# An encoder block of twelve attention units: rows of narrow heads in two halves of the partitions, one pool of PSUM banks, another order of loads and steps

## What is computed

```python
x = x + 0.5 * ffn(layernorm(x)); x = x + attn(layernorm(x)); x = x + 0.5 * ffn(layernorm(x))
# attn: 16 heads of dimension 4, on the left 64 channels
q, k, v = (left @ W.T).reshape(N, S, 16, 4); att = softmax(q k / sqrt(8)); out = (att v) @ Wo.T + bo
# ffn: 16 heads of dimension 8 with rope, then RMS norm, a shared MLP, a group and expert router, 8 experts
q = rope(src @ Wq); k = rope(src @ Wk_c @ Wk); v = src @ Wv_c @ Wv
x = rmsnorm(src + softmax(q k / sqrt(8)) v @ Wo, n1)
h = swiglu(x @ W1_shared); routed = sum_e (h @ W2[e]) * w[:, e]      # w: the best 2 of 4 experts of one group
out = rmsnorm(x + swiglu(x @ W_shared_in) @ W_shared_out + routed, n2)
```

## Time and profile before

| | us |
|---|---|
| median of 3 runs (lowest, highest) | 1025.39 (1023.57, 1027.55) |
| span of the profiled execution | 1017.9 |
| PE busy in it | 914.7 (90%) |
| DVE busy | 716.2 (70%) |
| ACT busy | 536.3 (53%) |
| POOL busy | 349.8 (34%) |
| granted PE clock, mean | 0.947 of 2.4 GHz |

### The profile page before, as it was taken

How to read it: one execution, slowest core, us unless ns; L and a number is a source line. 1 busy time by engine, 2 the same in 40 slices (tenths; PEclk the granted TensorE clock), 3 DMA queues, 4 the chain that set the end, 5 groups by cost and what they waited for, 6 DMA issues and landing times.

```text
span 1017.9 us, 12955 instructions
## 1 busy us (share of the span) xinstructions
PE 914.7 (90%) x4228; PEld 328.1 (32%) x4308; DVE 716.2 (70%) x1344; ACT 536.3 (53%) x1062; POOL 349.8 (34%) x669
## 2 busy tenths in 40 slices
PE   2179988999999999999999999999989999999967
PEld 1022223433433333333322323223233433433333
DVE  6579868768768666865867878778777688683227
ACT  1003755547537545653667666666754367367421
...
GB/s 166 102 80 56 71 61 24 79 30 1 34 13 47 33 8 51 11 27 7 50 42 43 23 96 22 63 67 30 100 2 67 63 13 3 1 13 3 1 10 10
DMA packets 21733, 41.28 MB, mean 41 GB/s; under 512 B 3308, under 2 KB 19500, under 8 KB 20012
## 3 DMA queue, kind: packets, MB, share of 16 engines
...
q10 hardware_dynamic: 240, 0.10, 0.0%
...
## 4 chain that ended last, share of the span: by engine, by line
PE 67%; DMA 9%; DVE 8%; issue 6%; POOL 5%; ACT 4%; SPq 1%; POOLq 0%; ACTq 0%; DVEq 0%
PE ps_max L552 14%; PE ps_out L587 14%; PE ps_exp L574 12%; PE ps L648 9%; PE ps L633 5%; DMA qk_parts<-parts 4%; DMA max_parts_rows<-maxT 3%; DVE maxes L726 2%; ACT probs L884 2%; PE ps L599 2%; DVE src L755 2%; PE ps L534 2%; PE ps L611 1%; PE ps L640 1%; PE ps_max L648 1%
## 5 line engine op out<-in xcount | busy, mean ns | idle before, releaser
L884 ACT ACTIVATE probs<-ps_exp 128x512 f32<-128x512 f32 x768 | 434.6, 594 | 298.4 <-PE ps_exp L574 247.4
L726 DVE TENSOR_REDUCE maxes<-ps_max 128x1 f32<-128x512 f32 x768 | 494.3, 684 | 132.0 <-PE ps_max L552 130.3
L552 PE MATMUL ps_max<-k_aug,q_aug 72*128 72x512 bf16 (+1 forms) x768 | 306.3, 401 | 25.8 <-DMA k_aug<-ones_row 12.5
L574 PE MATMUL ps_exp<-q_aug,k_aug 128*128 128x512 bf16 x688 | 265.7, 389 | 16.3 <-DMA q_aug<-max_parts_rows 9.2
L587 PE MATMUL ps_out<-probs,v_aug 128*9 128x512 f32 x1536 | 204.2, 604 | 4.0 <-ACT probs L884 2.2
L552 PEld LDWEIGHTS ps_max<-k_aug,q_aug 72*128 72x128 bf16 (+1 forms) x768 | 74.7, 98 | 265.9 <-DVE maxes L726 141.9
L574 PEld LDWEIGHTS ps_exp<-q_aug,k_aug 128*128 128x128 bf16 x768 | 74.9, 98 | 181.8 <-ACT probs L884 91.9
L648 PE MATMUL ps<-w,hidden 128*128 128x512 f32 x216 | 101.8, 599 | 0.0
L815 DVE TENSOR_TENSOR prod<-ps,gate 128x512 f32<-128x512 f32 x52 | 36.0, 692 | 55.3 <-PE ps L648 43.4
L1078 POOL TENSOR_TENSOR prod<-prod 128x512 f32<-128x512 f32 x28 | 35.5, 1268 | 97.7 <-DVE prod L815 83.0
L963 POOL TENSOR_SCALAR var_eps<-mean_var 128x4 f32<-128x4 f32 x12 | 2.8, 233 | 162.0 <-DVE mean_var L686 162.0
...
## 6 DMA issues: line engine op xcount, KB each, us to landing
...
qk_parts<-parts SPq DMA_DIRECT2D x48, 128.0 KB, 2.3
...
```

The source lines that it names most:

```text
L552: pe.matmul(ps_max[:, n % MAX_RING, :], q_aug[0:k, r, h, qt * 128:(qt + 1) * 128], k_aug[0:k, r, h, :], start=True, stop=True).then_inc(ma ...
L574: pe.matmul(ps_exp[:, n % EXP_RING, :], k_aug[:, r, h, kt * 128:(kt + 1) * 128], q_aug[:, r, h, :], start=True, stop=True).then_inc(exp_fu ...
L726: dve.tensor_reduce(maxes[:, u % 2, h // HH, qt, h % HH:h % HH + 1], ps_max[:, n % MAX_RING, :], AX.X, ALU.max).then_inc(max_done, 1)
L884: act.activation(probs[:, step % P_RING, c, :], ps_exp[:, n % EXP_RING, :], ACT.Exp, scale=scale).then_inc(exp_done, 1)
```

## The change

- **Banks.** All seven banks besides `ps_out` are one pool. `plan()` gives each step the banks that come free first by a table of holding times (`HOLD`).
- **Row halves.** In an attention unit half of the heads have their rows at partitions 0 to 38 and half at 64 to 102 (`first_row`), and consecutive matmuls change between the halves. `exp_scores` reads product rows plus 3 only, so no row is set to zero.
- **Head order and `v_aug`.** Heads go in groups of four; `v_aug` has 18 columns per head, of which 9 are zero, so two groups add up in one `ps_out`. Per unit there are two evacuations (L892 before) instead of four, and 8 transposes of heads instead of 16. The maxima are transposed in one go per piece, and there are two or four pieces per unit (`EARLY_UNITS`).
- **Loads.** q rows come by one DMA instead of three, k rows by three that each take every third row. For unit 0 they come in four pieces of four heads, k stored and loaded by ACT's queue. The 19 late weights are issued one by one among the steps. Rows of ones are loaded only where they move.
- **Last unit.** Its queries go in two halves; the work after the first half stands among the exponentials of the second.
- **Places.** Every table of places is new, and `MAX_LATE` is a list, one number per unit.

```diff
+def first_row(u, h):
+    return 64 * half_of(u, h)
+def group_head(g, c):
+    return 8 * (g // 2) + 2 * c + g % 2
+MAX_LATE = [39, 33, 23, 14, 16, 18, 22, 24, 25, 21, 15, 18, 14]
+def max_place(u, m):
+    start, end = ((v - 1) * TILES + MAX_LATE[v] for v in (u, u + 1))
+    if u and (is_ffn(u) != is_ffn(u - 1) or u in MAX_PAIRS):
+        m += 1 - m % 2
+    return start + m * (end - start) // TILES
...
+    def take(self, name, u, place):
+        run = max_run(u) if name == "max_scores" else exp_run(u) if name == "exp_scores" else 1
+        n = 2 if name in TWO_BANKS else run if name in HOLD else 0
+        taken = sorted(sorted(range(BANKS), key=lambda i: self.free_at[i])[:n])
...
+            for g, i in itertools.product(range(halves), range(pieces)):
+                r0, at = first_row(u, 2 * g), slice((g + i) * n, (g + i + 1) * n)
...
+                    of = of.rearrange("d c h n -> (d c) h n").unsqueeze(1)
+                    queue.dma_start(q_aug[r0:r0 + rows, r, at, :], of.to_broadcast([PARTS * d, PARTS, n, S])).then_inc(landed, 16)
...
-                    pe.matmul(ps_exp[:, n % EXP_RING, :], k_aug[:, r, h, kt * 128:(kt + 1) * 128],
-                              q_aug[:, r, h, :], start=True, stop=True).then_inc(exp_full, 1)
+                        pe.matmul(bank(use[i]), k_aug[p0:p1, r, at, kt * 128:(kt + 1) * 128],
+                                  q_aug[p0:p1, r, at, :], start=True, stop=True).then_inc(bank_full[use[i][0]], 1)
...
-                        mm = pe.matmul(ps_out[COL * c:COL * c + VW, :], v_aug[:, r, kt, h * VW:(h + 1) * VW],
-                                       probs[:, n % P_RING, c, :], start=(kt == 0), stop=(kt == TT - 1))
+                        mm = pe.matmul(ps_out[COL * c:COL * c + 2 * VW, :], v_aug[:, r, kt, 4 * (g // 2) + c, x0:x0 + 2 * VW],
+                                       probs[:, n % P_RING, c, :], start=first_one, stop=last_one)
...
-                    if u < 2:
-                        if u == 0:
-                            seq(pool.memset(k_aug[64:128, 0:1, :, :].bitcast(F32), 0.0))
```

785 lines of the change are left out of this document (491 added, 294 removed).

## The result

The changed kernel takes 863.53 us (median of 4 runs, 861.74 to 864.27) against 1024.74 us (1023.57 to 1027.55): a ratio of 0.843, 95% interval 0.841 to 0.846. The forecast was 884 us with a range of 862 to 916. The result is faster, as forecast, and lies at the lower edge of the range: the gain is 161 us where 141 were forecast. The profiled execution took 863.97 us, its span is 862.2 us.

A forecast was written before the change was run, and what follows sets the result against it. PE's queue was taken to bound stages 1 to 10, and chains of single steps the opening and tail. Opening, stages and tail summed to 877 us of span; 7.5 more gave 884 us, range 862 to 916.

The forecast's parts named there:

- The span and the runs: Whole kernel: the span lies 7.5 us below the median of the runs, so a span of 877 means 884 us.
- The opening: Before the first exponential: faster row loads and 28 reductions ahead instead of 49 give 47 us instead of 88.3.
- PE's queue: Stages 1 to 10: summed instruction prices on PE give queues such as 78, 76 and 73.5 us for stages 1 to 3.
- The allowance above the queue: Ffn stages carry 2 to 3 us above PE's queue; stages 7 and 8 take 56 and 57 for queues of 51 and 54.
- The wait in stages 1 and 9: Stages 1 and 9: 8 us of waiting for rows behind q loads shrinks, leaving them 3 us above their queues.
- Stages 5 and 6: Attention stages: PE, DVE and ACT each have 40 to 42 us, tied by banks, giving 49 each; ends 43 and 60.
- Rival "evacuation bounds them": Attention stages: evacuation and shared banks hold stages 5 and 6 at 58, 7 and 8 at 59; 910 us, chance 0.15.
- The halves overlap: Pairs of 36-row matmuls in different halves run together, saving 4.9 us in stage 3, 10 in stage 4, 6 in stage 7.
- the rival: Stages 3 to 7: matmuls in different row halves don't overlap; 31 us more, 915 us, chance 0.15.
- Late weights: Stage 0: 19 weights queued among row loads cost nothing, covered by unit 1's early rows; otherwise one wait up to 9.86 us.
- Stage 11 and tail: End of the kernel: stage 11 takes 70 us and the tail 34 instead of 48, together 104 instead of 117.
- The slower case: All 1536 score matmuls wait for planned banks; slower than before above 0.09 us each, 1068 us at 0.12; chance 0.02.

The follow-up runs named there:

- experiment 8: Changed kernel with unit 0's rows loaded whole instead of in four pieces of four heads: 871.12 us against 863.53.
- experiment 7: Changed kernel with the max matmuls of every unit back at 15 places behind the start of the stage before: 956.14 us against 863.53.
- experiments 1 and 2: Changed kernel with both row halves at partition 0: 900.96 us; changed kernel without rounding max matmul places to pairs in units 4 and 8: 883.26 us.
- experiment 6: Changed kernel with the seven banks divided between max scores, exponentials and the rest as in the kernel before: 908.05 us against 863.53.
- experiment 9: Changed kernel with each of the eight transposes of a unit's heads done twice on PE: 869.26 us against 863.53.
- Experiment 10: Changed kernel with every eighth reduction on DVE done twice, the second into a spare column: 889.15 us against 863.53.
- experiment 1: Changed kernel with all narrow heads of attention units at partition 0 instead of half at 64: 900.96 us against 863.53.
- Experiments 3 and 4: Changed kernel with the 19 late weights issued at the very beginning: 859.39 us; changed kernel with them 32 places later: 860.22 us.
- Experiment 5: Changed kernel with the last unit not cut into two halves of its queries, post work at the old places: 879.65 us against 863.53.

## Why the prediction was right, and where it was not

**The span and the runs.** I set the time 7.5 above the span, as in the kernel before. Here run and span differ by 1.8 (863.97 and 862.2), and in 21 later executions of the kernel before by 1.9 to 2.6, so the profiled execution there must have been some 5 us faster than the median. Of the 20 us by which the forecast was high this is 6; the stages give the other 15.

**The opening**, forecast 47 us: 47.0, and the first max matmul at 30.1 for 28. The mechanism holds in both its halves. The store of k parts is slower the more of q loads beside it (experiment 8), and fewer reductions ahead do bring the first exponential forward (15.9 us by experiment 7). The hit to the tenth is luck: the first max matmul came 2.1 us late, and what follows it took 16.9 us where 19 were put. The working led by 28 reductions; 16 and the way of the row stand on the path.

**PE's queue.** The forecast's queue sums for stages 1 to 3 and 7 to 10 are 78, 76, 73.5, 51, 54, 75, 73; measured are 79.4, 77.2, 75.0, 51.8, 53.2, 76.2, 72.7. That is within 1.5 us. Pairs and changes of tile are confirmed in experiments 1 and 2. Stage 4 took 72.7 where the queue had 68 and the forecast 71: in its first 15 us DVE is busy for 14.5 us and PE for 13.2, so there DVE leads, which the forecast had only for stages 5 and 6. One price was wrong: a transpose is 0.11, not 0.22, so the 8 fewer per unit save 0.9 and not 1.8 us a stage. It also makes every sum too long, by 0.9 us for the eight of heads alone, so part of the agreement is two errors that meet; PE's own idle time in these stages is 0.2 to 1.1 us.

**The allowance above the queue.** I put 2 to 3 us on each ffn queue "like stage 2" of before, and 5 and 3 on those of stages 7 and 8. The stages came out between 0.8 below and 1.5 above their sums. This is the term that was mis-sized, and it is what stages 1 to 3 and 7 to 10 came out shorter, 15.5 us (7 and 8 alone 8). With divided banks and all the rest in place the same stages stand 2 to 8 us above the same sums (experiment 6): sharing the banks takes away waits that I had priced at nothing. Experiment 6 puts sharing at 44 us. That is its price with all the rest in place, not a share of the gain: the new order was laid out for shared banks, and in the kernel before, with divided ones, PE waited for a bank for only 1 us or so of stage 2. The same holds for the places (some 90 us in experiment 7). The prices of taking parts away (25, 20, 12, 44, 90 and 8) add up to more than the 161 gained.

**The wait in stages 1 and 9.** I had taken the 8 us of stage 1 above its sum for a wait behind the loads of q rows, and the forecast's drop to 3 above the queue rests on it. The trace of before doesn't bear this out: within stages 1 and 9 PE waits for no DMA. (At the end of stages 7 and 8 it does wait, 2.20 and 3.39 us, for a row of maxima.) What it waits for is VectorE's norm; before, then now:

```profile
166.70 4.47 DVE L755 SCALAR_TENSOR_TENSOR src<-src,rms,n 128x128 f32<-128x128 f32 x4
...
171.23 1.12 PE L618 MATMUL ps<-ident,src 128*128 128x128 f32 x4 [2.49 <-DVE src L755]
```
```profile
126.95 1.12 DVE L1002 SCALAR_TENSOR_TENSOR src<-src,rms,n 128x128 f32<-128x128 f32 x4
```

The four instructions took 4.47 us while POOL worked on 128x512 tiles beside them, and take 1.12 now with POOL idle, as they took 1.14 in the tail of before. Behind the wait of 2.49 us the clock was 0.56 for 7 us, which is 3.1 us of work, and in the first 5 us of stage 1 it was 0.56 too, another 2.2, behind a wait of 3.59 us for a row of maxima at the end of stage 0. The stages came out 1.4 and 1.2 above their sums, less than the 3 forecast, so the size was nearly right and its reason was not: that is luck. No run separates the place of the norm from the other edits.

**Stages 5 and 6**, forecast 49 each: 47.1 and 47.3, with DVE at 89 and 94%. The stages stand 3 to 5 us above DVE's busy time, less than the 7 that I chose between 1 and 18. Rival "evacuation bounds them" was right that PE is not alone there (experiment 9: 0.9 us more on PE lengthens stage 5 by 0.5 and stage 6 not at all) and wrong in the size, 58 us. Experiment 10 can't be read by stage, so what more work on DVE costs there isn't shown.

**The halves overlap.** Forecast at 0.60, the rival at 0.15 with 31 us; experiment 1 measures 25. The Trainium skill's "Measured speedup vs the span model" (page "TensorE: Matmul & The Clock Gate") has 3.07 times for four row tiles; by my estimate from it a pair would have cost 0.29 (the prediction has 0.28). Two starts together, the next two 0.23 us behind them, and stage 7 within 1 us of its queue show no such loss for two halves.

**Late weights.** I took nothing and named the price should the cover go, up to 9.86. The cover I named (unit 1's rows, 28 us ahead of their use) held; what was hit was another thing, the rows of maxima of unit 0, and stage 0 took 62.7 us instead of 56. Experiments 3 and 4 give 5.8 and 5.4 of it back. Both beat the changed kernel; the better is 859.4 us.

**Stage 11 and tail**, forecast 70 and 34: 66.7 and 33.2. The tail went step by step: the norm 11.4 (11.7), logits 3.5 behind it (1.5), the router from there 8.0 (10.6), multiply-adds 6.1 (6.1), the end 4.1 (4). PE's queue of stage 11 was overcounted by 3 us. Experiment 5 puts the split at 12 to 16 us (13 forecast).

**The slower case** (each score matmul waits over 0.09 us for its named bank) did not come: PE idles 0.7 us before all 75 max matmuls of stage 1.

**What stays open**: which stages the extra reductions of experiment 10 lengthen, what sharing is worth in the attention stages, and what lets the clock fall in stage 4.
